# Attention and a gated FFN on one core: orders searched anew, and the last residual split between two engines

## The reference

```python
xn = layernorm(x)                                  # over the 256 features, no weights
q, k, v = (xn @ W.T, 16 heads of 16, for W in (Wq, Wk, Wv))
att = q @ k.T / sqrt(16) + causal mask             # 512 x 512 per head
s = (softmax(att) @ v) @ Wo.T
gate = silu(qlinear(xn, wq_gate, s_gate))          # 256 -> 704, W = (wq - 128) * scale
g = silu(qlinear(gate * qlinear(xn, wq_up, s_up), wq_down, s_down))   # 704 -> 256
out = x + s * g
```

## Time and profile before

| | us |
|---|---|
| median of three runs | 263.68 |
| the profiled execution | 263.83 |
| its span in the trace | 262.1 |
| TensorE busy | 254.9 |
| VectorE busy | 216.0 |
| ScalarE busy | 180.9 |
| GpSimd busy | 154.7 |

### The profile page before, as it was taken

The page is one execution under the profiler, slowest core; times in us unless marked ns, Lnnn a source line. Parts: engine busy times, 40 slices in busy tenths (PEclk is TensorE's granted clock), DMA queues, the critical chain, the costliest instruction groups (busy, mean ns, idle before and its releaser), DMA issues.

```text
span 262.1 us, 5867 instructions
## 1 busy us (share of the span) xinstructions
PE 254.9 (97%) x1976; PEld 191.9 (73%) x1976; DVE 216.0 (82%) x694; ACT 180.9 (69%) x340; POOL 154.7 (59%) x249
## 2 busy tenths in 40 slices
PE   8999989999999999999999999999999999999993
PEld 8788779876667668769666786868776768668782
DVE  7899997979878899877999868988799779997244
ACT  2876663678879855739779777655677887867750
POOL 6698982169565831585548780454538666773440
PEclk9999999999999999999999999999999999999998
DMA  7977233305151762275660102408724200124002
GB/s 255 326 223 181 61 81 105 102 11 114 44 123 45 157 180 78 52 172 142 182 193 3 41 5 63 102 27 207 179 82 94 76 23 24 40 72 140 0 3 80
DMA packets 20245, 26.77 MB, mean 102 GB/s; under 512 B 3384, under 2 KB 11512, under 8 KB 20216
## 3 DMA queue, kind: packets, MB, share of 16 engines
q1 hardware_dynamic: 19560, 25.35, 35.6%
q10 hardware_dynamic: 656, 1.05, 1.1%
HBM read 7.61 MB, written 2.10 MB: 37 GB/s over the span
## 4 chain that ended last, share of the span: by engine, by line
PE 80%; DVE 8%; ACT 4%; POOL 4%; issue 1%; ACTq 1%; POOLq 0%
PE ps L445 17%; PE ps L447 13%; PE ps L446 13%; PE ps L606 12%; PE ps L589 9%; PE ps L571 8%; PE ps L451 3%; DVE ps L1053 3%; POOL hid L865 3%; PE ps L488 1%; ACT hid L752 1%; DVE zbuf L1071 1%; POOL hl L869 1%; ACT hid L760 1%; DVE u L1106 1%
## 5 line engine op out<-in xcount | busy, mean ns | idle before, releaser
L1053 DVE CUSTOM_DVE_ANT_0 ps<-ps,maskt 128x512 f32<-128x512 f32 (+3 forms) x256 | 117.9, 524 | 21.4 <-PE ps L571 20.9
L815 ACT ACTIVATE pt<-ps 128x512 f32<-128x512 f32 x160 | 84.9, 603 | 16.7 <-PE ps L589 14.5
L899 POOL TENSOR_SCALAR_AFFINE_SELECT pt<-pt 128x256 f32<-128x256 f32 (+1 forms) x112 | 47.8, 442 | 72.7 <-ACT pt L815 72.0
L606 PE MATMUL ps<-pt,vt 128*32 128x256 f32 (+3 forms) x528 | 37.8, 427 | 0.3 <-DVE mx L1053 0.3
L1053 DVE DVE_READ_ACCUMULATOR2_ANT mx<- 128x1 f32 x256 | 36.4, 142 | 0.1
L865 POOL TENSOR_TENSOR hid<-hid 128x512 f32<-128x512 f32 x24 | 32.0, 1338 | 4.2 <-DVE hid L1032 2.5
L589 PE MATMUL ps<-qp,kp 64*128 64x512 f32 (+3 forms) x256 | 32.7, 341 | 0.0
L571 PE MATMUL ps<-kp,qp 64*128 64x512 f32 (+3 forms) x256 | 32.3, 340 | 0.0
L606 PEld LDWEIGHTS ps<-pt,vt 128*32 128x32 f32 x528 | 15.5, 109 | 21.6 <-issue 16.6
L869 POOL TENSOR_TENSOR hl<-hid,hh 128x512 fp32r<-128x512 f32 x20 | 25.9, 1302 | 4.2 <-ACT hh L768 4.1
L445 PE MATMUL ps<-xh,guh 128*128 128x512 f32 x66 | 28.2, 428 | 0.0
(11 more groups left out here) (132 smaller groups left out, 504.9 us busy)
## 6 DMA issues: line engine op xcount, KB each, us to landing
qp<-stg SPq DMA_DIRECT2D x42, 128.0 KB
kp<-stg SPq DMA_DIRECT2D x39, 128.0 KB
zbuf<-zbuf SPq DMA_DIRECT2D x28, 128.0 KB, 2.8
xr<-in_x SPq DMA_DIRECT2D x4, 512.0 KB, 3.7
out<-xr SPq DMA_DIRECT2D x8, 256.0 KB, 2.3
xin<-in_x SPq DMA_DIRECT2D x3, 512.0 KB, 3.9
pt<-in_wgT SPq DMA_DIRECT2D x1, 704.0 KB, 6.3
pt<-in_wuT SPq DMA_DIRECT2D x1, 640.0 KB, 7.6
```

The source lines that it names most:

```text
L606: mm = nc.tensor.matmul(ps[32 * a:32 * a + VC, bank, at:end], vt[:, j, VC * (GH * g + a):VC * (GH * g + a + 1)], pair(b, 5 * g + kk)[:, e, ...
L815: nc.scalar.activation(pair(b, s)[:, e, :], ps[:, BANKS["s", b, s][e], :], ACT.Exp, scale=SCALE).then_inc(exp_done[e], 1)
L899: mm = nc.gpsimd.affine_select(out=diag, in_=diag, compare_op=ALU.is_ge, fill=0.0, base=0, pattern=[[0, diag.shape[1]], [1, P]], channel_m ...
L1053: mm = nc.vector.tensor_tensor_reduce(part, part, maskt[:, T - wide:], -1.0, TOP, ALU.add, ALU.min, mg[:, e, a // 2, i:i + 1])
```

## The change

All five orders are replaced by others with the same units, save for the last residual. In batch 3, `res:3:0` moves from VectorE's list to the end of GpSimd's, and `sout:3:0` from SP's list to the end of ScalarE's. The units' code is the same, but for a wait in SP's store and the new store of ScalarE:

```diff
             def store_out(b, n):                      # SP
                 if b == B - 1:
-                    w.need("last", last_out_done, n + 1)
+                    w.need("last", last_out_done, 1)
                 else:
                     w.need("res", out_done, 2 * b + n + 1)
...
+            def store_out(b, n):                      # ScalarE
+                w.need("out", out_done, 2 * b + n + 1)
+                act_e.dma_start(out[b].rearrange("(i p) d -> p i d", p=P)[:, 2 * n:2 * n + 2, :],
+                                xr[:, 2 * n:2 * n + 2, :]).then_inc(out_stored, 16)
```

The ends of the lists (VectorE, GpSimd, SP, ScalarE):

```diff
-norm:3:2 u:3:1 norm:3:3 norm:3:4 zlo:3:1 zlo:3:2 fin:3:0 res:3:0 fin:3:1 res:3:1
+norm:3:2 u:3:1 norm:3:3 norm:3:4 zlo:3:1 zlo:3:2 fin:3:0 fin:3:1 res:3:1
-mask:3:15 zm:3:0 mask:3:16 mask:3:17 mask:3:18 mask:3:19 zlo:3:0
+mask:3:15 zm:3:0 mask:3:16 mask:3:17 mask:3:18 mask:3:19 zlo:3:0 res:3:0
-zrow:2:2 crow:3:0 zrow:2:3 crow:3:1 zrow:3:0 crow:3:2 sout:2:0 sout:2:1 zrow:3:1 loadres:3:0 crow:3:3 sout:3:0
-sout:3:1
+zrow:2:2 crow:3:0 zrow:2:3 crow:3:1 zrow:3:0 crow:3:2 sout:2:0 sout:2:1 zrow:3:1 loadres:3:0 crow:3:3 sout:3:1
-zhi:3:0 fth:3:1 zcp:3:3 zcp:3:4 zhi:3:1 zhi:3:2
+exq:3:19 zhi:3:0 fth:3:1 zcp:3:3 zcp:3:4 zhi:3:1 zhi:3:2 sout:3:0
```

TENSOR_ORDER from batch 2's last scores to batch 3's third (banks and all), before and after:

```diff
-gu:3:4:3 m:3:3:01 pv:2:2:4 m:3:4:02 s:2:15:35 s:2:16:67 gu:3:5:4 m:3:5:36 s:2:17:05 m:3:6:12 gu:3:6:7 c:3:0:0
-s:2:18:36 s:2:19:14 gu:3:7:2 gu:3:8:0 s:3:0:13 m:3:7:56 m:3:8:47 pv:2:3:2 s:3:1:13 s:3:2:45 m:3:9:67 gu:3:9:2
+gu:3:4:0 gu:3:5:6 s:2:15:17 m:3:3:23 m:3:4:45 pv:2:2:6 s:2:16:01 s:2:17:27 m:3:5:34 gu:3:6:5 m:3:6:06 s:2:18:23
+s:2:19:14 gu:3:7:7 gu:3:8:6 c:3:0:0 m:3:7:12 m:3:8:34 pv:2:3:5 m:3:9:07 s:3:0:12 s:3:1:34 gu:3:9:5 m:3:10:37
```

GPSIMD_ORDER in the same stretch:

```diff
-mask:2:12 mask:2:13 mask:2:14 hid:3:1 zm:2:0 hlo:3:1 zlo:2:0 mask:2:15 mask:2:16 hid:3:2 mask:2:17 hlo:3:2 mask:2:18
-mask:2:19 hid:3:3 mask:3:0 hlo:3:3 mask:3:1 mask:3:2 hid:3:4 mask:3:3 mask:3:4 hlo:3:4 zm:2:1 mask:3:5 zlo:2:1
+mask:2:12 mask:2:13 mask:2:14 zm:2:0 hid:3:1 hid:3:2 hlo:3:1 hlo:3:2 mask:2:15 zlo:2:0 mask:2:16 mask:2:17 mask:2:18
+mask:2:19 hid:3:3 hlo:3:3 mask:3:0 mask:3:1 hid:3:4 mask:3:2 hlo:3:4 mask:3:3 mask:3:4 zm:2:1 mask:3:5 zlo:2:1
```

More of the change, by code:

```diff
@@ L103 @@
[L103 to L107, removed]
@@ L118 @@
-maxb:3:16 fin:2:1 maxa:3:17 maxb:3:17 maxa:3:18 hlt:3:0 maxb:3:18 maxa:3:19 maxb:3:19 sh:3:3 rec:3:0 rec:3:1 u:3:0
-norm:3:2 u:3:1 norm:3:3 norm:3:4 zlo:3:1 zlo:3:2 fin:3:0 res:3:0 fin:3:1 res:3:1
+sh:0:0 maxa:0:5 maxb:0:5 maxa:0:6 maxb:0:6 maxa:0:7 qlo:0:3 maxb:0:7 maxa:0:8 maxb:0:8 u:0:0 maxa:0:9 xlo:1:0
+xlo:1:1 maxb:0:9 sh:0:1 u:0:1 bn:2:0 bn:2:1 bn:2:2 bn:2:3 mom:2:0 gate:1:0 maxa:0:10 maxb:0:10 qlo:1:0 gate:1:1
+maxa:0:11 maxb:0:11 maxa:0:12 maxb:0:12 maxa:0:13 maxb:0:13 maxa:0:14 maxb:0:14 sh:0:2 maxa:0:15 maxb:0:15 qlo:1:1
@@ new lines @@
+gate:1:2 maxa:0:16 maxb:0:16 gate:1:3 maxa:0:17 maxb:0:17 maxa:0:18 maxb:0:18 maxa:0:19 maxb:0:19 sh:0:3 gate:1:4
+maxa:1:0 maxb:1:0 maxa:1:1 maxb:1:1 rec:0:0 rec:0:1 qlo:1:2 maxa:1:2 maxb:1:2 qlo:1:3 gate:1:5 maxa:1:3 maxb:1:3
+maxa:1:4 maxb:1:4 sh:1:0 maxa:1:5 maxb:1:5 hlt:1:0 xlo:2:0 maxa:1:6 maxb:1:6 xlo:2:1 maxa:1:7 maxb:1:7 maxa:1:8
+maxb:1:8 maxa:1:9 maxb:1:9 qlo:2:0 rec:0:2 rec:0:3 sh:1:1 gate:2:0 qlo:2:1 bn:3:0 bn:3:1 bn:3:2 bn:3:3 mom:3:0
+maxa:1:10 maxb:1:10 maxa:1:11 maxb:1:11 qlo:2:2 fin:0:0 fin:0:1 maxa:1:12 maxb:1:12 maxa:1:13 maxb:1:13 maxa:1:14
@@ new lines @@
+maxb:1:14 sh:1:2 u:1:0 maxa:1:15 maxb:1:15 u:1:1 maxa:1:16 maxb:1:16 maxa:1:17 maxb:1:17 gate:2:1 maxa:1:18
+maxb:1:18 qlo:2:3 maxa:1:19 maxb:1:19 sh:1:3 maxa:2:0 maxb:2:0 maxa:2:1 maxb:2:1 gate:2:2 rec:1:0 rec:1:1 gate:2:3
+maxa:2:2 maxb:2:2 gate:2:4 maxa:2:3 maxb:2:3 maxa:2:4 maxb:2:4 sh:2:0 maxa:2:5 maxb:2:5 maxa:2:6 maxb:2:6 maxa:2:7
+maxb:2:7 maxa:2:8 maxb:2:8 gate:2:5 xlo:3:0 xlo:3:1 hlt:2:0 maxa:2:9 maxb:2:9 sh:2:1 qlo:3:0 rec:1:2 gate:3:0
+maxa:2:10 maxb:2:10 rec:1:3 maxa:2:11 maxb:2:11 maxa:2:12 maxb:2:12 maxa:2:13 maxb:2:13 qlo:3:1 maxa:2:14 maxb:2:14
@@ L120 @@
+maxb:3:16 maxa:3:17 fin:2:1 hlt:3:0 maxb:3:17 maxa:3:18 maxb:3:18 maxa:3:19 maxb:3:19 sh:3:3 rec:3:0 rec:3:1 u:3:0
+norm:3:2 u:3:1 norm:3:3 norm:3:4 zlo:3:1 zlo:3:2 fin:3:0 fin:3:1 res:3:1
 """
 GPSIMD_ORDER = """
-init3:0:0 rows:0:3 rows:0:4 sc:0:0 rows:0:5 vones:0:0 hid:0:0 hid:0:1 hlo:0:0 hlo:0:1 hid:0:2 hid:0:3 hlo:0:2
-hlo:0:3 root:1:0 root:1:1 hid:0:4 hid:0:5 hlo:0:4 root:1:2 root:1:3 mask:0:0 mask:0:1 mask:0:2 mask:0:3 root:2:0
-root:2:1 root:2:2 root:2:3 mask:0:4 hid:1:0 hid:1:1 hlo:1:0 hlo:1:1 mask:0:5 hid:1:2 mask:0:6 hlo:1:2 mask:0:7
@@ L125 @@
-mask:0:8 mask:0:9 hid:1:3 mask:0:10 hlo:1:3 mask:0:11 mask:0:12 mask:0:13 mask:0:14 hid:1:4 zm:0:0 mask:0:15 hlo:1:4
-zlo:0:0 hid:1:5 mask:0:16 mask:0:17 mask:0:18 mask:0:19 mask:1:0 mask:1:1 mask:1:2 mask:1:3 zm:0:1 zlo:0:1 hid:2:0
-root:3:0 mask:1:4 root:3:1 root:3:2 root:3:3 mask:1:5 res:0:0 mask:1:6 res:0:1 mask:1:7 mask:1:8 mask:1:9 hlo:2:0
-mask:1:10 mask:1:11 mask:1:12 hid:2:1 mask:1:13 hlo:2:1 hid:2:2 mask:1:14 zm:1:0 hlo:2:2 hid:2:3 mask:1:15 zlo:1:0
-mask:1:16 mask:1:17 hlo:2:3 hid:2:4 mask:1:18 mask:1:19 hlo:2:4 hid:2:5 mask:2:0 mask:2:1 mask:2:2 mask:2:3 zm:1:1
@@ L130 @@
-mask:2:4 zlo:1:1 hid:3:0 mask:2:5 res:1:0 res:1:1 mask:2:6 mask:2:7 mask:2:8 mask:2:9 hlo:3:0 mask:2:10 mask:2:11
-mask:2:12 mask:2:13 mask:2:14 hid:3:1 zm:2:0 hlo:3:1 zlo:2:0 mask:2:15 mask:2:16 hid:3:2 mask:2:17 hlo:3:2 mask:2:18
-mask:2:19 hid:3:3 mask:3:0 hlo:3:3 mask:3:1 mask:3:2 hid:3:4 mask:3:3 mask:3:4 hlo:3:4 zm:2:1 mask:3:5 zlo:2:1
-hid:3:5 mask:3:6 mask:3:7 res:2:0 mask:3:8 mask:3:9 res:2:1 mask:3:10 mask:3:11 mask:3:12 mask:3:13 mask:3:14
-mask:3:15 zm:3:0 mask:3:16 mask:3:17 mask:3:18 mask:3:19 zlo:3:0
+init3:0:0 vones:0:0 sc:0:0 rows:0:3 rows:0:4 rows:0:5 hid:0:0 hid:0:1 hlo:0:0 hlo:0:1 hid:0:2 hid:0:3 hlo:0:2
@@ new lines @@
+hlo:0:3 root:1:0 root:1:1 hid:0:4 hid:0:5 hlo:0:4 root:1:2 root:1:3 mask:0:0 mask:0:1 root:2:0 root:2:1 mask:0:2
+root:2:2 root:2:3 mask:0:3 mask:0:4 hid:1:0 hid:1:1 hlo:1:0 mask:0:5 hlo:1:1 mask:0:6 mask:0:7 hid:1:2 mask:0:8
+mask:0:9 hlo:1:2 hid:1:3 mask:0:10 hlo:1:3 mask:0:11 mask:0:12 hid:1:4 mask:0:13 mask:0:14 zm:0:0 mask:0:15 zlo:0:0
+hlo:1:4 mask:0:16 hid:1:5 mask:0:17 mask:0:18 mask:0:19 mask:1:0 mask:1:1 mask:1:2 mask:1:3 zm:0:1 hid:2:0 zlo:0:1
+root:3:0 mask:1:4 root:3:1 root:3:2 root:3:3 res:0:0 res:0:1 mask:1:5 mask:1:6 mask:1:7 mask:1:8 hlo:2:0 mask:1:9
@@ new lines @@
+hid:2:1 mask:1:10 hlo:2:1 mask:1:11 mask:1:12 mask:1:13 hid:2:2 mask:1:14 hlo:2:2 zm:1:0 hid:2:3 zlo:1:0 hlo:2:3
+mask:1:15 mask:1:16 hid:2:4 mask:1:17 mask:1:18 hlo:2:4 mask:1:19 hid:2:5 mask:2:0 mask:2:1 mask:2:2 zm:1:1 mask:2:3
+mask:2:4 zlo:1:1 hid:3:0 mask:2:5 res:1:0 mask:2:6 res:1:1 mask:2:7 mask:2:8 mask:2:9 hlo:3:0 mask:2:10 mask:2:11
+mask:2:12 mask:2:13 mask:2:14 zm:2:0 hid:3:1 hid:3:2 hlo:3:1 hlo:3:2 mask:2:15 zlo:2:0 mask:2:16 mask:2:17 mask:2:18
+mask:2:19 hid:3:3 hlo:3:3 mask:3:0 mask:3:1 hid:3:4 mask:3:2 hlo:3:4 mask:3:3 mask:3:4 zm:2:1 mask:3:5 zlo:2:1
@@ L135 @@
+hid:3:5 mask:3:6 mask:3:7 mask:3:8 res:2:0 mask:3:9 res:2:1 mask:3:10 mask:3:11 mask:3:12 mask:3:13 mask:3:14
+mask:3:15 zm:3:0 mask:3:16 mask:3:17 mask:3:18 mask:3:19 zlo:3:0 res:3:0
 """
 SYNC_ORDER = """
-init4:0:0 loadx:1:0 pkh:0:0 pkl:0:0 pkh:0:1 pkl:0:1 pkh:0:2 pkl:0:2 pkh:0:3 pkl:0:3 loadres:0:0 crow:0:0 loadx:2:0
-crow:0:1 pkh:1:0 pkl:1:0 zrow:0:0 crow:0:2 pkh:1:1 pkl:1:1 zrow:0:1 crow:0:3 pkh:1:2 pkl:1:2 pkh:1:3 zrow:0:2
-pkl:1:3 loadx:3:0 crow:1:0 zrow:0:3 pkh:2:0 crow:1:1 pkh:2:1 pkl:2:0 pkl:2:1 zrow:1:0 sout:0:0 pkh:2:2 pkl:2:2
```

123 lines of the change are left out of this document (59 added, 64 removed).

## The result

The changed kernel takes 264.91 us (264.67 to 265.07, six runs) against 263.47 us (263.14 to 263.85, six runs) of the kernel before on the same chip: 1.0053 times as long, 95% interval 1.0040 to 1.0066. It is slower by 1.4 us; the forecast was 262.1, its range ended at 263.5. The profiled execution took 264.95 us, its span 263.2.

A forecast was written before the change was run, and what follows sets the result against it. The prediction took the time as TensorE's units in written order plus a tail. From the profiled 263.83 us, -1.56 for the order, 0 for waits and 0 for the tail gave 262.27, 262.1 as a median; range 261.0 to 263.5.

The forecast's parts named there:

- TensorE's order, -1.56: TensorE's unit order: twelve fewer changes of unit kind, six visits fewer at 0.26 us each, saves 1.56 us.
- six visits: TensorE's trips from 64 rows to the 128-row array and back, saved by the new order; 0.22 to 0.31 us each.
- TensorE's real waits: TensorE's waits for other engines: taken as unchanged, 0, with bounds of -1.5 and +1.5 us.
- The other orders: New orders on VectorE, ScalarE, GpSimd and SP: cost only through TensorE's waits, 0.
- The tail: Last residuals and stores at the kernel's end: the end moves between -0.40 and +0.3 us, taken as 0.
- Given back by new waits: Rival: grouped 64-row units bring bank refills nearer their readers, TensorE's waits double, +1.5, 263.6 us; chance 0.13.
- VectorE: Rival: VectorE's run from 211 to 239 us sets the end, 8 of 12 places count, 262.6 us; chance 0.18.
- GpSimd in batch 2: Rival: five GpSimd jobs ahead of a mask delay value unit pv:2:3, 264.8 us as a median; chance 0.09.

The follow-up runs named there:

- the bare run: Kernel before plus unread projections and 64-row units behind TensorE's last unit, in blocks, then alternating; trace only: alternating takes 1.86 us more for five visits, 0.37 each.
- the mended kernel: Kernel after with GpSimd's and VectorE's start lists as in before and banks refitted from gu:0:7 to the last scores: 262.32 us, 0.9961.
- the run with both mended: Kernel after with GpSimd's and VectorE's start lists as in before and only the banks from gu:0:7 to m:0:7 refitted: 263.25 us, 0.9999.
- the later renumbering: Kernel after, same orders, only bank numbers from da:0:0 to the last scores changed to those the trace shows free first: 263.96 us, 1.0020.
- the run with more visits: Kernel before with projections and 64-row units interleaved at seven places in TensorE's order, nine visits more, banks refitted: 274.64 us, 1.0409.

## Why the prediction was wrong

The view was right: TensorE sets the time, and the spacing of its units is what an order changes.

TensorE's order, -1.56: right in kind, low in size. The table has -1.74, the medians over all traces -2.3 and six visits at the 0.37 of the bare run -2.2; the 128-row side of a visit was read rightly (0.22, in the bare run 0.21), the 64-row side was read at one of its two borders (0.09, in the bare run 0.16). Between the start and batch 3 TensorE's time did shrink, by 0.7 us (m:0:7 to m:3:0, 40.14 + 110.34 before, 39.26 + 110.48 after). That the mended kernel comes out at 262.32, close to the forecast, is in part chance: it saves more by its spacing than the 1.56 and still waits longer than before.

TensorE's real waits, 0 with bounds of 1.5: this is the step that failed. They grew by 3.28 us by the table (3.8 by the medians over all traces), and this ate the whole saving. It read: "The last is the start of batch 0's second half: the GpSimd products and VectorE's hlt ahead of it stand in the same order as before, and the same units lie before it on TensorE, so it stays." The products do stand in the same order, but not what GpSimd and VectorE do ahead of and between them: the first five units of GpSimd and several of VectorE had changed places, and with the banks that cost 1.4 us (the run with both mended). Nor did I follow the bank digits. That "the units between a producer and its consumer mostly keep their number" looked at the data; a unit waits as well for the last reader of its bank, and the later renumbering alone is worth 0.9 (1.0 once the start is mended).

The other orders, 0: wrong by the same step. That "their orders cost only through TensorE's waits" holds; I did not then count those waits.

The tail, 0: right (264.85 against 264.91). The last residual took 0.92 us, not 1.11: the row that I leaned on lay beside 0.56 us of GpSimd's instruction, this one beside 0.37. It was not the only row of its kind either, as VectorE's `wdl` meets GpSimd's products in the start of before as well. The second store was issued 260.36 - 258.65 = 1.71 after TensorE's last matmul, where I had said about 1.8 (1.85 before); the span still ends 0.1 later, and that store took 2.4 us to land, where the two of before took 2.1.

The rivals. "Given back by new waits" was the mechanism, down to "bring each bank's refill nearer to its reader"; it had 0.13 of the chance and a price of 1.5, under half of what came: near what the later waits cost, without the start's. "VectorE" did not decide: it is busy 19.45 of 20 us from 220 to 240, but the waits there shrank with the banks, at the same work; what is left of them is the open point below. "GpSimd in batch 2" did not come: pv:2:3 starts 0.72 us after m:3:7, the spacing of two 64-row units, with no wait before it:

```profile
211.51 0.79 PE L570 MATMUL ps<-kp,qp 64*128 64x384 f32 x8
212.23 1.07 PE L605 MATMUL ps<-pt,vt 128*32 128x512 f32 x8
```

What stays open: the 0.4 us each at m:3:15 and s:3:10 that the mended kernel still waits, for banks whose last reader is VectorE (at m:3:15 VectorE and ScalarE, which end together); no other bank was free there, and other orders of those units were not tried.

## What to carry to other kernels

When lists are replaced, read each list's head for what now stands ahead of the first long chain, and price buffers as well as data: for every unit, ask who read its bank last and when that was done. A saving in one engine's own spacing is kept only if its refills still have slack; choosing the buffer that the trace shows free first costs nothing and was worth 0.9 us here. Two late things in a row hide each other: test mends together before dropping one that gives nothing alone.

## What the hardware showed that was not expected

A visit costs 0.37 us when single units alternate: (6 x 1.57 - 8.39) / 5 = 0.21 on the projections (8.39 = 296.95 - 288.56), the rest on the 64-row units. In the run with more visits a wait of TensorE of 2.1 us was followed by 3.4 us at the lower clock, which cost 1.7 us more.

When VectorE works on two SBUF tiles beside a GpSimd product, the one that starts later is lengthened by what is left of the other's instruction, less 0.13 to 0.16 us. Five meetings show it. `wdl` in after starts at 21.07 with 0.93 left of the product (20.71 + 1.29 = 22.00) and takes 2.28 instead of 1.49, 0.79 more. `wol` at 25.31 has 0.87 left (24.46 + 1.72 = 26.18) and takes 0.74 more. VectorE's `hlt` has 0.56 left and takes 0.43 more. The last residual has 0.37 left (258.52 + 1.26 = 259.78, against a start at 259.41) and takes 0.92 instead of 0.69. The other way round, the GpSimd product at 21.89 has 0.80 left of `wdl` (21.20 + 1.49 = 22.69) and takes 1.95 instead of 1.31. The one that was there first kept its length in these five, but for the `hl` at 24.46: it also met the end of `wdl`'s second part (23.27 + 1.51 = 24.78), and its 1.72 is about 0.24 more than that explains.
